# Routing of a macaron block: softplus ahead of the ranks, and a counter of its own for the ranks

## The reference

```
x = x + 0.5 * ffn(layernorm(x))       # pass "p" of the kernel
x = x + attention(layernorm(x))       # 16 heads of 16, window of 64 positions
x = x + 0.5 * ffn(layernorm(x))       # pass "q", the same weights as p

ffn(X):
  shared  = silu(X @ sW1 + sb1) @ sW2 + sb2
  logits  = X @ routing_W.T + expert_bias          # 8 experts
  act     = sqrt(softplus(logits))
  combine = act where it is among the 2 largest of its row, else 0
  routed  = sum over e of combine[:, e] * (silu(X @ rW1[e] + rb1[e]) @ rW2[e] + rb2[e])
  return shared + routed
```

## Time and profile before

| | |
|---|---|
| time before, median of 3 runs | 1568.67 us (1567.11 to 1570.02) |
| the profiled execution's own time | 1562.98 us |
| its span | 1561.1 us |
| PE busy | 1506.6 us, 97% |
| DVE busy | 1186.7 us, 76% |
| ACT busy | 1127.8 us, 72% |
| POOL busy | 790.8 us, 51% |
| mean granted TensorE clock | 0.986 of full speed |

### The profile page before, as it was taken

The page is one execution under the profiler, slowest core; times in us unless marked ns, Lnnn a source line. Parts: engine busy times, 40 slices in busy tenths (PEclk is TensorE's granted clock), DMA queues, the critical chain, the costliest instruction groups (busy, mean ns, idle before and its releaser), DMA issues.

```text
span 1561.1 us, 41431 instructions
## 1 busy us (share of the span) xinstructions
PE 1506.6 (97%) x13969; PEld 1359.6 (87%) x13969; DVE 1186.7 (76%) x4773; ACT 1127.8 (72%) x3416; POOL 790.8 (51%) x794
## 2 busy tenths in 40 slices
PE   7898999999999999999999999999999999999898
PEld 7787889898888989899898988988898898998787
DVE  6857687878868787887878788787878888886554
ACT  5467687877777787787778777777867778686733
POOL 4434455645555464555455455554545554554333
PEclk9998999999999999999999999999999999999899
DMA  3063536344363644545363454546345353635200
GB/s 118 15 203 103 148 120 186 106 137 133 119 170 96 188 119 131 136 125 168 104 187 112 137 130 135 157 119 177 109 138 141 119 159 108 174 108 155 84 28 14
DMA packets 264392, 199.66 MB, mean 128 GB/s; under 512 B 150859, under 2 KB 220918, under 8 KB 264182
## 3 DMA queue, kind: packets, MB, share of 16 engines
q1 hardware_dynamic: 263972, 196.94, 43.8%
q0 software_dynamic: 32, 0.07, 0.0%
q10 hardware_dynamic: 178, 0.02, 0.0%
HBM read 141.86 MB, written 42.43 MB: 118 GB/s over the span
## 4 chain that ended last, share of the span: by engine, by line
PE 59%; DVE 15%; SPq 8%; issue 7%; ACT 5%; DMA 5%; POOL 2%; DVEq 0%; POOLq 0%; ACTq 0%
PE gb L1048 8%; PE gb L1050 8%; PE gb L1049 8%; PE yb L1048 6%; PE yb L1050 5%; PE yb L1049 5%; PE ptb L1121 4%; PE sb_ L1112 4%; SPq L570 4%; PE cxb L1140 3%; ACT pr L717 2%; SPq L565 2%; PE gb L1162 2%; DVE pr L920 1%; DVE ag L998 1%
## 5 line engine op out<-in xcount | busy, mean ns | idle before, releaser
L664 POOL TENSOR_TENSOR gl<-ag,gh 128x512 fp32r<-128x512 f32 x288 | 376.2, 1309 | 267.2 <-ACT gh L762 266.1
L647 POOL TENSOR_TENSOR pr<-pr,rinv 128x512 f32<-128x512 f32 x256 | 274.4, 1074 | 279.5 <-DVE rinv L928 276.6
L717 ACT ACTIVATE pr<-pr,mx 128x128 f32<-128x128 f32 x1024 | 396.4, 391 | 8.7 <-DVE mx L920 6.6
L1048 PE MATMUL yb<-w2h,gh 128*128 128x256 f32 x1152 | 334.7, 291 | 10.5 <-POOL gl L664 10.4
L1050 PE MATMUL yb<-w2l,gh 128*128 128x256 f32 x1152 | 321.7, 279 | 0.0
L1049 PE MATMUL yb<-w2h,gl 128*128 128x256 f32 x1152 | 321.6, 279 | 0.0
L775 ACT ACTIVATE tt<-gb,b1half 128x512 f32<-128x512 f32 x288 | 195.3, 680 | 130.1 <-PE gb L1050 125.9
L920 DVE CUSTOM_DVE_ANT_0 pr<-sb_,mask 128x128 f32<-128x128 f32 x1024 | 235.4, 285 | 36.8 <-issue 25.8
L992 DVE SCALAR_TENSOR_TENSOR ag<-gb,b,gate 128x512 f32<-128x512 f32 x256 | 190.0, 744 | 89.3 <-ACT tt L775 55.7
L1048 PE MATMUL gb<-xh,w1h 128*128 128x512 f32 x576 | 243.2, 422 | 1.7 <-DVE ag L992 1.3
L762 ACT ACTIVATE gh<-ag 128x512 fp32r<-128x512 f32 x288 | 179.9, 625 | 88.3 <-DVE ag L998 68.1
(11 more groups left out here) (154 smaller groups left out, 2827.3 us busy)
## 6 DMA issues: line engine op xcount, KB each, us to landing
gate<-gates_pair SPq DMA_DIRECT2D x240, 256.0 KB, 3.8
ks<-qk_dram SPq DMA_DIRECT2D x256, 128.0 KB, 2.9
qs<-qk_dram SPq DMA_DIRECT2D x512, 64.0 KB, 2.5
qk_dram<-qkh SPq DMA_DIRECT2D x64, 256.0 KB, 2.4
qk_dram<-qkl SPq DMA_DIRECT2D x64, 256.0 KB, 2.7
vb<-va SPq DMA_DIRECT2D x32, 384.0 KB, 6.1
xres<-L_attn_x_dram SPq DMA_DIRECT2D x16, 512.0 KB, 4.6
out_dram<-xres SPq DMA_DIRECT2D x16, 512.0 KB, 4.1
```

What stands on the lines that cost most here:

```text
L647: nc.gpsimd.tensor_tensor(pr[:, k], pr[:, k], rinv[:, k, :].unsqueeze(2).to_broadcast([P, NP, P]), ALU.mult).then_inc(a_pn, 1)
L664: nc.gpsimd.tensor_tensor(gl[:, k, :], ag[:, k, :], gh[:, k, :].bitcast(F32), ALU.subtract).then_inc(f_gl, 1)
L717: nc.scalar.activation(pr[:, k, r, :], pr[:, k, r, :], ACT.Exp, bias=mx[:, k, r:r + 1], scale=-1.0, accum_out=rsum[:, k, r:r + 1]).then_in ...
L1048: nc.tensor.matmul(dst, ah, bh, start=start, stop=False, **kw)
```

## The change

In every pass's DVE order the names `Lq` and `R1` trade places, so that `softplus` is issued ahead of `ranks`. What stood between the two stays where it was. `ranks` counts on a new semaphore `f_rk`, 5 a pass; `f_rt` then counts 7 for `logits` and 9 for `softplus`, 16 in all, and POOL's `zz`, which waits for the full number of `f_rt`, no longer waits for `ranks`. `R2` gets a wait for `f_rk`. No operation is added or taken away.

```
@@ ORDER, DVE @@
-... pg6-4 qLr-6 qLq-6 qR1-6 pa7-4 ...
+... pg6-4 qLr-6 qR1-6 qLq-6 pa7-4 ...
-... axl1-4 pLr-3 pLq-3 ql00-4 ql01-4 pR1-3 qa5-6 ...
+... axl1-4 pLr-3 pR1-3 ql00-4 ql01-4 pLq-3 qa5-6 ...
@@ HEAD and TAIL: the same trade in every pass @@
...
-        f_lg, f_rt, f_en, f_sq, f_cf, f_ct, f_cth, f_cr, f_g1 = (
+        f_lg, f_rk, f_rt, f_en, f_sq, f_cf, f_ct, f_cth, f_cr, f_g1 = (
...
-        NRANK = 12
+        NRANK = 7
         NRT = NRANK + 9
...
-            def chain(n, at):
+            def chain(n, at, count=f_rt, every=NRT):
 
-                done = [NRT * n + at]
+                done = [every * n + at]
 
                 def op(ins):
                     done[0] += 1
-                    ins.then_inc(f_rt, 1)
-                    dve.wait_ge(f_rt, done[0])
+                    ins.then_inc(count, 1)
+                    dve.wait_ge(count, done[0])
                 return op
...
             def ranks(n):
 
-                op = chain(n, 7)
+                op = chain(n, 0, f_rk, 5)
...
                 elif s[1:] == "R2":
                     n = nth(s, b)
                     dve.wait_ge(f_sq, n + 1)
+                    dve.wait_ge(f_rk, 5 * n + 5)
                     wait(dve, f_ct, n)
```

More of the change, by code:

```diff
@@ L36 @@
     "DVE": """
-qxl1-6 pg5-4 ri6-5 pa6-4 pg6-4 qLr-6 qLq-6 qR1-6 pa7-4 mx7-5 pg7-4 pa8-4 qR2-6 pg8-4 ri7-5 mx8-5 qa0-6 mx9-5
+qxl1-6 pg5-4 ri6-5 pa6-4 pg6-4 qLr-6 qR1-6 qLq-6 pa7-4 mx7-5 pg7-4 pa8-4 qR2-6 pg8-4 ri7-5 mx8-5 qa0-6 mx9-5
 qg0-6 ri8-5 mx10-5 ri9-5 pT-4 aN1-4 mx11-5 qa1-6 qg1-6 ri10-5 qa2-6 pxl0-3 qg2-6 mx12-5 pxl1-3 ctl0-5 qa3-6
-axl0-4 qg3-6 qa4-6 ri11-5 qg4-6 ri12-5 axl1-4 pLr-3 pLq-3 ql00-4 ql01-4 pR1-3 qa5-6 qg5-6 mx13-5 pR2-3
+axl0-4 qg3-6 qa4-6 ri11-5 qg4-6 ri12-5 axl1-4 pLr-3 pR1-3 ql00-4 ql01-4 pLq-3 qa5-6 qg5-6 mx13-5 pR2-3
 mx14-5 ri13-5 qa6-6 ql10-4 qg6-6 mx15-5 vl0-4 ri14-5 ri15-5 qa7-6 qg7-6 qa8-6 qg8-6 pa0-3 ql11-4 pg0-3 mx0-4
@@ L88 @@
     "DVE": """
-pN1=0 Wlrw=0 Wl1s=0 pxl0=0 pxl1=0 Wl1r=0 pLr=0 pLq=0 pR1=0 Wl2r=0 Wl2s=0 pR2=0 pa0=0 Wl1t=0 pg0=0 pa1=0
+pN1=0 Wlrw=0 Wl1s=0 pxl0=0 pxl1=0 Wl1r=0 pLr=0 pR1=0 pLq=0 Wl2r=0 Wl2s=0 pR2=0 pa0=0 Wl1t=0 pg0=0 pa1=0
 pg1=0 pa2=0 Wl2t=0 pg2=0 pa3=0 Wb=0 pg3=0 Wlvo=0 Wlqk=0 pa4=0 pN1=1 pg4=0 pa5=0 pg5=0 pa6=0 pg6=0 pa7=0
-pg7=0 pa8=0 pxl0=1 pg8=0 pxl1=1 pLr=1 pLq=1 pT=0 pa0=1 aN1=0 pg0=1 pR1=1 pN1=2 pR2=1 axl0=0 axl1=0 ql00=0
+pg7=0 pa8=0 pxl0=1 pg8=0 pxl1=1 pLr=1 pR1=1 pT=0 pa0=1 aN1=0 pg0=1 pLq=1 pN1=2 pR2=1 axl0=0 axl1=0 ql00=0
 ql01=0 vl0=0 pa1=1 pg1=1 pa2=1 pg2=1 vl1=0 ql10=0 ql11=0 pa3=1 pg3=1 pa4=1 pg4=1 pa5=1 pg5=1 pa6=1 mx0=0
 pg6=1 mx1=0 ri0=0 mx2=0 ri1=0 ri2=0 mx3=0 mx4=0 ri3=0 pa7=1 mx5=0 pg7=1 ri4=0 pa8=1 mx6=0 pg8=1 ri5=0 pxl0=2
-mx7=0 ri6=0 pxl1=2 ri7=0 pLr=2 mx8=0 pLq=2 pR1=2 pT=1 mx9=0 ri8=0 aN1=1 mx10=0 ri9=0 pa0=2 ctl0=0 pg0=2
+mx7=0 ri6=0 pxl1=2 ri7=0 pLr=2 mx8=0 pR1=2 pLq=2 pT=1 mx9=0 ri8=0 aN1=1 mx10=0 ri9=0 pa0=2 ctl0=0 pg0=2
 mx11=0 ri10=0 pR2=2 mx12=0 ri11=0 axl0=1 mx13=0 axl1=1 ri12=0 mx14=0 ri13=0 ri14=0 mx15=0 ql00=1 ql01=1
 ri15=0 pa1=2 vl0=1 pg1=2 ql10=1 ql11=1 pa2=2 ctl1=0 pg2=2 pa3=2 aR0=0 pg3=2 aR1=0 qN1=0 vl1=1 pN1=3 mx0=1
-pa4=2 pa5=2 pg4=2 pg5=2 mx1=1 ri0=1 qxl0=0 qxl1=0 mx2=1 ri1=1 qLr=0 ri2=1 mx3=1 qLq=0 pa6=2 ri3=1 mx4=1
-qR1=0 mx5=1 ri4=1 pg6=2 pa7=2 pg7=2 ri5=1 mx6=1 qR2=0 mx7=1 ri6=1 pa8=2 qa0=0 pg8=2 qg0=0 ri7=1 mx8=1 mx9=1
+pa4=2 pa5=2 pg4=2 pg5=2 mx1=1 ri0=1 qxl0=0 qxl1=0 mx2=1 ri1=1 qLr=0 ri2=1 mx3=1 qR1=0 pa6=2 ri3=1 mx4=1
+qLq=0 mx5=1 ri4=1 pg6=2 pa7=2 pg7=2 ri5=1 mx6=1 qR2=0 mx7=1 ri6=1 pa8=2 qa0=0 pg8=2 qg0=0 ri7=1 mx8=1 mx9=1
 ri8=1 pT=2 ri9=1 aN1=2 qa1=0 ctl0=1 qg1=0 qa2=0 qg2=0 pxl0=3 mx10=1 qa3=0 qg3=0 pxl1=3 mx11=1 ri10=1 axl0=2
-axl1=2 pLr=3 pLq=3 ri11=1 pR1=3 mx12=1 ql00=2 ql01=2 qa4=0 mx13=1 qg4=0 ri12=1 pR2=3 ri13=1 qa5=0 qg5=0
+axl1=2 pLr=3 pR1=3 ri11=1 pLq=3 mx12=1 ql00=2 ql01=2 qa4=0 mx13=1 qg4=0 ri12=1 pR2=3 ri13=1 qa5=0 qg5=0
 mx14=1 ql10=2 qa6=0 mx15=1 qg6=0 ri14=1 qa7=0 qg7=0 ri15=1 vl0=2 qa8=0 qg8=0 ql11=2 pa0=3 pg0=3 mx0=2 qT=0
@@ L183 @@
     "DVE": """
-qxl1=10 pg5=12 ri6=11 pa6=12 pg6=12 qLr=10 qLq=10 qR1=10 pa7=12 mx7=11 pg7=12 pa8=12 qR2=10 pg8=12 ri7=11
+qxl1=10 pg5=12 ri6=11 pa6=12 pg6=12 qLr=10 qR1=10 qLq=10 pa7=12 mx7=11 pg7=12 pa8=12 qR2=10 pg8=12 ri7=11
 mx8=11 qa0=10 mx9=11 qg0=10 ri8=11 mx10=11 ri9=11 pT=12 aN1=12 qa1=10 ri10=11 qg1=10 mx11=11 ctl0=11 qa2=10
 qg2=10 pxl0=13 pxl1=13 mx12=11 qa3=10 qg3=10 ri11=11 axl0=12 mx13=11 axl1=12 ri12=11 mx14=11 qa4=10 qg4=10
-ri13=11 ri14=11 ql00=12 ql01=12 pLr=13 pLq=13 pR1=13 qa5=10 qa6=10 qg5=10 qg6=10 ql10=12 mx15=11 pR2=13
+ri13=11 ri14=11 ql00=12 ql01=12 pLr=13 pR1=13 pLq=13 qa5=10 qa6=10 qg5=10 qg6=10 ql10=12 mx15=11 pR2=13
@@ L188 @@
 qa7=10 vl0=12 qg7=10 ri15=11 qa8=10 qg8=10 ql11=12 pa0=13 mx0=12 pg0=13 ri0=12 qT=10 mx1=12 ctl1=11 mx2=12
 ri1=12 vl1=12 ri2=12 aR0=11 mx3=12 pa1=13 pg1=13 aR1=11 ri3=12 mx4=12 qN1=11 pa2=13 ri4=12 pg2=13 pa3=13
-mx5=12 pg3=13 pN1=14 pa4=13 pg4=13 ri5=12 mx6=12 pa5=13 qxl0=11 qxl1=11 pg5=13 ri6=12 mx7=12 qLr=11 qLq=11
-qR1=11 ri7=12 pa6=13 pg6=13 pa7=13 qR2=11 pg7=13 pa8=13 mx8=12 pg8=13 qa0=11 mx9=12 qg0=11 ri8=12 ri9=12
+mx5=12 pg3=13 pN1=14 pa4=13 pg4=13 ri5=12 mx6=12 pa5=13 qxl0=11 qxl1=11 pg5=13 ri6=12 mx7=12 qLr=11 qR1=11
@@ L192 @@
+qLq=11 ri7=12 pa6=13 pg6=13 pa7=13 qR2=11 pg7=13 pa8=13 mx8=12 pg8=13 qa0=11 mx9=12 qg0=11 ri8=12 ri9=12
 pT=13 mx10=12 aN1=13 pxl0=14 qa1=11 ri10=12 qg1=11 qa2=11 ctl0=12 qg2=11 pxl1=14 mx11=12 qa3=11 qg3=11
-ri11=12 axl0=13 mx12=12 qa4=11 axl1=13 qg4=11 mx13=12 ri12=12 ri13=12 ql00=13 mx14=12 ql01=13 pLr=14 pLq=14
-pR1=14 ri14=12 qa5=11 qa6=11 qg5=11 qg6=11 pR2=14 ql10=13 mx15=12 qa7=11 vl0=13 qg7=11 ri15=12 qa8=11 qg8=11
+ri11=12 axl0=13 mx12=12 qa4=11 axl1=13 qg4=11 mx13=12 ri12=12 ri13=12 ql00=13 mx14=12 ql01=13 pLr=14 pR1=14
@@ L195 @@
+pLq=14 ri14=12 qa5=11 qa6=11 qg5=11 qg6=11 pR2=14 ql10=13 mx15=12 qa7=11 vl0=13 qg7=11 ri15=12 qa8=11 qg8=11
 mx0=13 ql11=13 pa0=14 pg0=14 ri0=13 mx1=13 qT=11 ri1=13 ctl1=12 vl1=13 mx2=13 aR0=12 mx3=13 ri2=13 pa1=14
 aR1=12 pg1=14 mx4=13 qN1=12 pa2=14 ri3=13 pg2=14 pN1=15 pa3=14 ri4=13 pg3=14 pa4=14 mx5=13 pg4=14 qxl0=12
-qxl1=12 mx6=13 ri5=13 pa5=14 pg5=14 ri6=13 pa6=14 qLr=12 pg6=14 qLq=12 qR1=12 pa7=14 mx7=13 pg7=14 pa8=14
+qxl1=12 mx6=13 ri5=13 pa5=14 pg5=14 ri6=13 pa6=14 qLr=12 pg6=14 qR1=12 qLq=12 pa7=14 mx7=13 pg7=14 pa8=14
@@ L203 @@
 pg2=15 ri4=14 pa3=15 pg3=15 mx5=14 pa4=15 pg4=15 pa5=15 ri5=14 pg5=15 mx6=14 qxl0=13 qxl1=13 pa6=15 ri6=14
-pg6=15 qLr=13 qLq=13 qR1=13 pa7=15 mx7=14 pg7=15 pa8=15 qR2=13 pg8=15 ri7=14 mx8=14 qa0=13 mx9=14 qg0=13
+pg6=15 qLr=13 qR1=13 qLq=13 pa7=15 mx7=14 pg7=15 pa8=15 qR2=13 pg8=15 ri7=14 mx8=14 qa0=13 mx9=14 qg0=13
 ri8=14 mx10=14 ri9=14 pT=15 aN1=15 qa1=13 ri10=14 qg1=13 ctl0=14 qa2=13 qg2=13 qa3=13 mx11=14 qg3=13 qa4=13
```

8 lines of the change are left out of this document (4 added, 4 removed).

## The result

The kernel after takes 1579.89 us (median of 8 runs, 1572.63 to 1585.36) where the kernel before takes 1567.46 us (8 runs, 1561.35 to 1570.02): ratio 1.0077, 95% interval 1.0059 to 1.0096. The change makes the kernel 0.6 to 0.8% slower, some 10 to 12 us.

What follows compares the result with a forecast made beforehand. DVE's queue behind q passes was taken to set PE's time, with no reserve, eleven times. Terms 4.6 + 1.1 - 1.2 + 1.0 + 2.3 + 0.9 + 0.6 = +9.3 us gave 1578.0 us; 8-in-10 range 1570.5 to 1586.

Steps and rivals of the forecast that it cites:

- Pass q in the middle: Eleven passes, q1 to q10 and q13: DVE stands 0.42 us for `exp`, delaying PE's scores each time; +4.6 us.
- The collision: Behind q5 or q13, the delayed L998 comes after POOL's `gl` and waits for it; one of two counted, +1.1 us.
- Pass p in the middle: `ql00` and `ql01` come about 0.3 us earlier, PE's `yb` waits shrink in four periods; -1.2 us.
- Pass p13: Nothing lies between the two steps and `exp` ends late: DVE stands 1.43 us, PE has some reserve; +1.0 us.
- Pass q14 and pass q15: q14: ranks, hidden in the `exp` wait before, delay R2, +2.3 us; q15: root wait goes but `gl` starts later, +0.6.
- Pass p1: Softplus waits for `exp`, so L1009, `pg0` and POOL's `gl`, for which PE waits, come 0.96 us later; +0.9 us.
- the rival of the lowered clock: Longer PE pauses in p1 and q14 lower the granted clock, 4 us more: 1582 us; chance 0.15.
- The root holds the ranks back: POOL's root keeps a rank operation out, up to 1.64 us more in each of eleven passes: 1596 us; chance 0.05.
- Faster: q passes cost nothing, and `yb` waits of the middle and R2's waits in first and last passes shrink: 1562.9 us; chance 0.09.
- no change: DVE catches up in the middle if `mx8` has another releaser; only tail and head cost: about 1569 us; chance 0.13.

Runs made afterwards that it cites:

- e_counter: Kernel after with ranks ahead of softplus again in all passes, keeping the separate semaphore and R2's added wait: 1566.5 us, ratio 0.9998 to the kernel before.
- r_after: The kernel after once more, unedited, with a second trace: 1577.0 us, ratio 1.0061 to the kernel before.
- e_head: Softplus ahead of ranks only in p0 to p3 and q0, old order elsewhere, separate counter kept: 1568.89 us, ratio 1.0023 to the kernel before.
- e_qall: Softplus ahead of ranks in all 16 q passes, old order in all p passes, separate counter kept: 1574.06 us, ratio 1.0048 to the kernel before.
- e_pall: Softplus ahead of ranks in all 16 p passes, old order in all q passes, separate counter kept: 1569.07 us, ratio 1.0018 to the kernel before.
- e_tail: Softplus ahead of ranks only in p13 to p15, q14 and q15, old order elsewhere, separate counter kept: 1570.98 us, ratio 1.0035 to the kernel before.
- e_p1: Softplus ahead of ranks in pass p1 alone, old order elsewhere, separate counter kept: ratio 1.0003 to the kernel before.
- e_cover1: Kernel after with the first of five rank operations issued right behind the logits, ahead of softplus, in every pass: 1574.14 us, ratio 1.0047 to the kernel before.

## Why the prediction was right, and where its terms were off

The forecast (1578.0, slower) was right, 1.9 us below the median, and the mechanism is the one it named: nothing but the order costs (e_counter), and the order costs because DVE stands still behind `exp`. The closeness is partly luck. The first comparison has +12.4 us between its medians, 3.1 more than the sum of +9.3, but its kernel before came out 1.2 us below the 1568.67 from which the forecast started. That the sum meets the 9.6 of r_after so well is luck too, for its terms err both ways. By the times the head was too cheap: e_head has +3.6 us [1.6, 5.6], where only the +0.9 of p1 stood. By the traces the tail was too cheap and the q passes of the middle too dear; by the times alone neither is outside its interval.

*Pass q in the middle* (+4.6). The mechanism was there: idle time of 0.28 us before L861, and window 9's scores 0.3 to 0.4 us later behind the logits than before in most passes. The 0.42 was a little too much, since DVE answers faster than the one row of q14 had it. ACT's `exp` of q4 in the kernel after:

```profile
570.34 0.21 ACT L747 ACTIVATE en<-en 128x8 f32<-128x8 f32 x1 [1.72 <-DVE en L842]
```

It ends at 570.55, and L861 starts 0.03 us later, not 0.09. What failed is the step from there to the end, "everything behind comes 0.42 later, and so do PE's scores": PE did lose 3.2 us in its scores, but gave 2.1 us of it back in the same periods at L1069. That wait stood mostly inside the duration of a matmul row; as idle time it was only some 0.5 us in nine periods. I had looked for PE's slack only in idle time. With one rank operation as cover the standstill was gone, and 1.0047 of 1.0061 stayed, within the intervals of both.

*The collision* (+1.1 for one of q5 and q13). It came at q13 and not at q5. DVE and POOL of the kernel after, in that order:

```profile
1397.64 1.79 DVE L999 SCALAR_TENSOR_TENSOR ag<-tt,ag 128x512 f32<-128x512 f32 x1
```

```profile
1397.61 1.27 POOL L664 TENSOR_TENSOR gl<-ag,gh 128x512 fp32r<-128x512 f32 x1 [4.08 <-ACT gh L762]
```

L999 started 0.03 us behind `gl` and took 1.79 us in place of 0.69. The scores behind q13 wait 1.99 us in e_qall and r_after alike, 0.54 in e_pall:

```profile
1391.52 0.66 PE L1113 MATMUL sb_<-ks,qs 128*128 128x128 f32 x4 [0.54 <-DVE mx L920]
```

*Pass p in the middle* (-1.2). Right in kind in one trace, and more: -3.6 us in nine periods of e_pall. Of that 1.7 us are idle time of PE. Beside the new order in q the gain is not seen. DVE in p7 of the kernel after, where L850 no longer stands under `gl`:

```profile
604.12 0.46 DVE L861 TENSOR_SCALAR zw<-en 128x8 f32<-128x8 f32 x1 [0.76 <-ACT en L747]
...
606.26 1.29 DVE L898 TENSOR_TENSOR qkl<-gb,qkh 128x512 fp32r<-128x512 f32 x2
...
607.46 0.42 DVE L850 TENSOR_TENSOR xn<-lg 128x256 f32<-128x256 f32 x1
```

*Pass p13* (+1.0): +0.9. DVE stood 1.29 us before L861.

*Pass q14 and pass q15* (+2.3 and +0.6): +3.6 together. The term of q14 is there to the tenth. Softplus starts 3.58 us behind L835 in e_counter and e_tail alike, and R2 (L964) starts 8.16 and 10.45 us behind it: 2.29 us later, the length of the ranks. The collision that was counted for q5 or q13 came here as well, 1.1 us more. DVE and POOL of e_tail:

```profile
1470.38 1.28 DVE L970 CAST cfs<-cfs 128x32 fp32r<-128x32 f32 x1
```

```profile
1470.36 1.26 POOL L664 TENSOR_TENSOR gl<-ag,gh 128x512 fp32r<-128x512 f32 x1 [3.62 <-ACT gh L762]
```

and DVE of e_counter, where `gl` starts at 1470.32, after R2's last operation has begun and all but ended:

```profile
1469.84 0.18 DVE L970 CAST cfs<-cfs 128x32 fp32r<-128x32 f32 x1
```

All six traces with the new order in q14 have this cast at 1.28 us. Of the six with the old order one has it too (e_p1), and in before L972 took 1.23 us. In e_counter and in e_tail C starts 0.05 to 0.06 us after R2 ends, so the clock has no part in the 3.4 us from L835 to C. In q15 R2 no longer waits for the root, as predicted, and Y0 waits 1.70 us for `gl` in e_tail, 1.02 in e_counter: the +0.6 of the prediction. In the kernel after and in e_qall that wait is 0.2 us, because PE comes there later.

*Pass p1* (+0.9): the wait for `gl` grew by 1.3 us. Of that DVE's delay is 0.93, as predicted; another 0.35 came on POOL, whose small operations ahead of `gl` now run beside the ranks (L630 took 1.19 us in e_p1, 1.01 in e_counter; L628 0.38 and 0.19). The clock added 1.5 us up to step C. This is the rival of the lowered clock, and it was no rival but an addition. Over six runs r_after has a mean granted clock of 0.981, the 29 runs of before 0.984. Over its span that is 10 us more at the lower level; among the runs of before, each us more there went with 0.27 us more time (0.21 to 0.22 in the two other sets). By these slopes a fifth to a quarter of the loss goes with the clock, an estimate from a correlation (0.69, 0.50 and 0.60).

*The root holds the ranks back* falls. The root started at 572.47 in q4 and L850 at 572.42, and all five rank operations kept 0.42 us. So it is in all eleven passes of the kernel after. What grew is the root, 1.64 to 1.87 us. The whole-instruction rule of the Trainium skill, SBUF — State Buffer, section "SBUF: two separate sides", by which this rival would have been the forecast, does not describe this pair; it does describe `gl` with L999.

*Faster* and *no change* fall too. The first had the place of the gain right (e_pall's middle), but not the price of p1 and p13, which take it back: the new order in all passes p alone gives 1.0018 [1.0003, 1.0033].

Open: what makes the stretch to step L of q14 1.0 us longer, since no wait in it stands out; whether p1's 2.6 us reach the end in full, as e_p1 alone came out at 1.0003; and how much of e_cover1's 1.0047 each place carries. Its trace still has a standstill of 1.0 us in p1, p13, p15, q14 and q15 and of 2.2 in p0, where one operation of 0.42 us is too short a cover. It reaches C of p1 at 80.91 us (76.84 with the old order), with the pause of 2.40 us and the lower clock there, and also with a lower-clock stretch in p0 that no other trace has. A kernel with the new order in p4 to p12 alone suggests itself (-3.6 us in one trace, without p1 and p13) and wasn't tried.

## What to carry to other kernels

An operation that stands between a question to another engine and the use of its answer is cover, even when it looks like an obstacle to what comes after: before moving it, ask what is queued behind the waiting instruction, not who wants the result sooner. A result delivered 2.3 us earlier to an engine that waits anyway is worth nothing. The same trade can pay in one pass and cost in another, so price it pass by pass, and look for slack also inside rows that are longer than their like. And at the thin places of a schedule (first and last passes) ask whether a longer pause of PE counts twice, as pause and as the clock behind it: in p1 it did.

## What was unexpected of the hardware

- At p1 a pause of PE of 1.01 to 1.06 us left the clock at its upper level in six of six traces, and one of 2.16 us did in one. Pauses of 2.29 to 2.40 us were followed by 3.4 us at the lower level in seven of seven, where matmuls of 0.28 us took 0.41 to 0.42. That is one place of one kernel.
- The small power on POOL (128 x 8 values) runs beside two-input VectorE operations without stopping them: these keep 0.42 us, the power goes from 1.64 to 1.87 us. `gl` (128 x 512) and L999 exclude one another: 1.79 us in place of 0.69. So do `gl` and a cast of 128 x 32 with one input (L970): 1.28 us in place of 0.18, started 0.02 us behind `gl`.
- L861, 8 values a partition, took 0.46 us in place of 0.17 in p7, where it started under a `gl` that ended at 604.55.
